# Row stage of a Hartley-transform convolution: from two column tiles of 64 rows to four of 32

## The reference

```python
# layer 0: a 3x3 filter whose taps come from the channel means, plus the input
lf = tanh(batchnorm(x.mean((2, 3)) @ conv_w.T)).reshape(N, G, 1, 9, 1)
low = sum(patches(x) * lf, axis=3).reshape(N, C, H, W)
x = (low * (inside_all + 1) - inside_all * gap) * lamb_l + x * (lamb_h + 1)
# layer 1: 20 x 20 modes of a 2-D Hartley transform, mixed over channels
x_ht = dht_2d(x)
out_ht[:, :, :20, :20] = compl_mul2d(x_ht[:, :, :20, :20], w1)
y = dht_2d(out_ht) / (H * W)
y = gaussian_smoothing_4d(y)      # 9 taps along images, channels, rows, columns
return y * (abs(fftfreq(W)) <= 0.25)
```

## Time and profile before

| | us |
|---|---|
| median of 3 runs | 151.3 |
| lowest and highest | 150.71 and 153.71 |
| the profiled execution, whole time | 152.74 |
| its span, first to last instruction | 150.9 |

### The profile page before, as it was taken

How to read it: one execution, slowest core, us unless ns; L and a number is a source line. 1 busy time by engine, 2 the same in 40 slices (tenths; PEclk the granted TensorE clock), 3 DMA queues, 4 the chain that set the end, 5 groups by cost and what they waited for, 6 DMA issues and landing times.

```text
span 150.9 us, 5209 instructions
## 1 busy us (share of the span) xinstructions
PE 125.7 (83%) x2308; PEld 71.9 (48%) x2308; DVE 79.8 (53%) x162; ACT 40.3 (27%) x92; POOL 55.3 (37%) x75
## 2 busy tenths in 40 slices
PE   6496558999999999999899797798797987999500
PEld 5132412655463626257567796465463654654200
DVE  0014840856497969595678114664846748444400
ACT  3000410011112020202599311343242423432300
POOL 8980000399876969699974000000000000000000
PEclk9999997589999999999999999999999999999995
DMA  3999999999999998000000000066998989999994
GB/s 99 358 359 321 295 347 362 348 349 372 371 363 380 351 351 273 11 2 4 0 2 0 4 4 4 4 213 242 312 365 300 384 300 329 350 376 380 386 386 158
DMA packets 34839, 37.04 MB, mean 245 GB/s; under 512 B 1162, under 2 KB 34260, under 8 KB 34816
## 3 DMA queue, kind: packets, MB, share of 16 engines
q1 hardware_dynamic: 34816, 36.70, 72.5%
HBM read 19.92 MB, written 16.78 MB: 243 GB/s over the span
## 4 chain that ended last, share of the span: by engine, by line
PE 28%; POOL 27%; DVE 13%; SPq 9%; DMA 9%; issue 8%; ACT 1%; POOLq 0%; DVEq 0%
PE ps L524 11%; POOL acc L870 5%; DMA x_ring<-x 5%; POOL rows L892 5%; SPq L315 5%; PE ps L464 4%; POOL spread L868 4%; PE ps L485 4%; DVE mixed L789 4%; PE ps L505 4%; DMA out<-rows 4%; DVE xht L726 4%; POOL row_prod L840 3%; POOL eo L878 2%; DVE rows L552 2%
## 5 line engine op out<-in xcount | busy, mean ns | idle before, releaser
L370 PE MATMUL ps<-x_ring,k_lt 64*64 64x512 f32 x256 | 34.7, 646 | 6.9 <-DMA x_ring<-x 6.9
L524 PE MATMUL ps<-cols,k_inv 128*64 128x330 f32 (+1 forms) x192 | 31.5, 466 | 4.5 <-DVE rows L552 4.0
L688 DVE STREAM_TRANSPOSE y_sb<-ps 128x1024 f32<-128x1024 f32 x16 | 19.5, 1241 | 18.2 <-PE ps L370 18.2
L524 PEld LDWEIGHTS ps<-cols,k_inv 128*64 128x64 f32 x192 | 13.3, 136 | 18.3 <-issue 11.8
L552 DVE COPY rows<-ps 128x330 f32<-128x330 f32 (+1 forms) x24 | 12.1, 522 | 12.1 <-PE ps L524 10.6
L388 PEld LDWEIGHTS ps<-y_sb,k_t 64*64 64x64 f32 x512 | 15.5, 143 | 5.0 <-DVE y_sb L688 2.7
L388 PE MATMUL ps<-y_sb,k_t 64*64 64x128 f32 x512 | 17.2, 288 | 0.4 <-ACT kb L589 0.4
L552 ACT COPY rows<-ps 128x330 f32<-128x330 f32 (+1 forms) x24 | 11.0, 462 | 23.7 <-PE ps L524 21.9
L370 PEld LDWEIGHTS ps<-x_ring,k_lt 64*64 64x64 f32 x256 | 8.7, 141 | 16.5 <-issue 9.1
L359 PE MATMUL ps<-idle 128*128 128x256 f32 x52 | 14.6, 431 | 1.2 <-DVE idle L657 1.2
L359 PEld LDWEIGHTS ps<-idle 128*128 128x128 f32 x52 | 10.5, 211 | 3.2 <-DVE idle L657 1.2
(11 more groups left out here) (70 smaller groups left out, 133.4 us busy)
## 6 DMA issues: line engine op xcount, KB each, us to landing
x_ring<-x SPq DMA_DIRECT2D x32, 512.0 KB, 8.7
out<-rows SPq DMA_DIRECT2D x16, 640.0 KB, 5.0
out<-rows SPq DMA_DIRECT2D x8, 768.0 KB, 6.2
w_sb<-mix_w SPq DMA_DIRECT2D x2, 960.0 KB, 10.1
k_inv<-inv SPq DMA_DIRECT2D x1, 386.0 KB, 8.6
k_t<-t SPq DMA_DIRECT2D x1, 256.0 KB, 7.2
k_basis<-basis SPq DMA_DIRECT2D x1, 240.0 KB
k_coef<-coef SPq DMA_DIRECT2D x4, 25.4 KB
```

The lines of the kernel that those rows point to most:

```text
L370: last = mm(ps[64 * m:64 * m + 64, 2 * hs + g, :], k_lt[64 * g:64 * g + 64, 64 * r:64 * r + 64], x_ring[64 * g:64 * g + 64, u, k:k + 4, r, ...
L524: last = mm(ps[64 * g:64 * g + 64, B_F[k % 3], 0:nt * NW], inv(O_LH + s * H + r * H // 2, (1, H // 2)), cols[:, u, 6 * g:6 * g + nt, :], s ...
L688: nc.vector.transpose(view(y_sb[:, n % 2, 0, 8 * hs, 0:1], (KINDS, 8), (KINDS * HC, 4), (1, 32)), view(ps[:, 2 * hs, 0:1], (1, 1024))).the ...
```

## The change

The row stage is cut four ways in place of two. A partition of `rows` now holds four image rows of 128 for each group of four channels. A chunk is made of four column tiles of 32 output partitions, one for each residue g of the channel number, and two halves (two image rows), so eight calls of `mm` in place of two, with half as many columns each: 3 x 66 = 198, or 2 x 66 = 132. The chunks become 396, 396, 396, 396, 264 and 264 columns, where they were 396, 396, 330, 330, 330 and 330. The tables, the order of the channels and the slices that `to_columns` takes follow the new layout; the copy has one dimension more. The stores are still three an image, of 3, 3 and 2 groups of four channels: 786, 786 and 524 KB, in runs of 2 KB.

```diff
-    order = np.arange(C).reshape(C // 2, 2).T.reshape(-1)
+    order = np.arange(C).reshape(C // 4, 4).T.reshape(-1)
-    wide[:, O_LH:O_TURN] = lh.reshape(3, 128, H // 2, 2).transpose(1, 0, 3, 2).reshape(128, -1)
+    wide[:, O_LH:O_TURN] = lh.reshape(3, 128, H // 4, 4).transpose(1, 0, 3, 2).reshape(128, -1)
-        rows = sb("rows", [128, 2, C // 2, 2, H])
+        rows = sb("rows", [128, 2, C // 4, 4, H])
-        CHUNKS = [(s, r, 6 if s == 0 else 5) for s in range(3) for r in range(2)]
+        CHUNKS = [(s, r, 3 if s < 2 else 2) for s in range(3) for r in range(2)]
-            out_pair = out.rearrange("n (k g) h w -> n k (g h w)", g=2).rearrange("n k (q e) -> n q k e", e=2 * H)
+            out_quad = out.rearrange("n (k g) h w -> n k (g h w)", g=4).rearrange("n k (q e) -> n q k e", e=4 * H)
-                    sp.dma_start(out_pair[n, :, s:HC:3, :],
-                                 rows[:, u, s:HC:3, :, :].rearrange("q k r w -> q k (r w)")
+                    sp.dma_start(out_quad[n, :, s:C // 4:3, :],
+                                 rows[:, u, s:C // 4:3, :, :].rearrange("q k r w -> q k (r w)")
-                    first = 3 * t * NF
+                    first = (t // 3 * 8 + t % 3 * 3) * NF
-                    for g in range(2):
-                        last = mm(ps[64 * g:64 * g + 64, B_F[k % 3], 0:nt * NW],
-                                  inv(O_LH + s * H + r * H // 2, (1, H // 2)),
-                                  cols[:, u, 6 * g:6 * g + nt, :], start=True, stop=True)
+                    for half in range(2):
+                        for g in range(4):
+                            last = mm(ps[32 * g:32 * g + 32, B_F[k % 3], half * nt * NW:(half + 1) * nt * NW],
+                                      inv(O_LH + s * H + (2 * r + half) * H // 4, (1, H // 4)),
+                                      cols[:, u, 3 * g:3 * g + nt, :], start=True, stop=True)
-            return copy(view(rows[:, u, s, r, 0:1], (3 * 2 * H, nt), (H - HALF, 2), (1, HALF)),
-                        view(ps[:, B_F[k % 3], 0:1], (NW, nt), (HALF, 2), (1, HALF)))
+            return copy(view(rows[:, u, s, 2 * r, 0:1], (H, 2), (3 * 4 * H, nt), (H - HALF, 2), (1, HALF)),
+                        view(ps[:, B_F[k % 3], 0:1], (nt * NW, 2), (NW, nt), (HALF, 2), (1, HALF)))
```

## The result

| | before | after |
|---|---|---|
| median of the runs, us | 152.24 (4 runs) | 164.44 (4 runs) |
| lowest and highest, us | 150.71, 153.71 | 162.62, 165.53 |
| span of the profiled execution, us | 150.9 | 162.3 |
| instruction packets | 18 | 22 |

The ratio is 1.085, with a 95% interval of 1.067 to 1.103: slower, as forecast, and 3 us beyond the range. The span grew by 11.4 us where the sum gave 6.4.

The account below looks back on a forecast made before the run. VectorE's chain (6.34 us an image) was taken as the bound until image 4, then the stores. With 7.8 us of PE stops, 145.2 + 8.5 + 3.6 gave a span of 157.3, median 157.7 us; range 152.3 to 161.5.

Parts of the forecast that it names:

- the sum: Whole kernel: last copy at 145.2, remaining stores 8.5, remainder 3.6, giving a span of 157.3 us, 6.4 over before.
- What bounds the kernel before: Inverse half: the chain through VectorE, 6.34 us an image, starves the stores (5.45 us) until image 4; then stores run solid.
- The runs of 2 KB: Output stores: 401 GB/s for 385, a gain of 0.7 us; rival that they don't help changes no verdict.
- The copy: VectorE's copy of a chunk: 570 ns at 396 columns for 498 at 330, +0.07 us on the chain.
- Four column tiles side by side: Row-stage matmuls on PE: four tiles overlap fully, so chunks 0 to 2 add only 0.12 us an image.
- The count: PE's instruction queue: 1152 more records, so 22 or 23 instruction packets for 18.
- mostly hidden: PE's borders between 256-instruction blocks: the skill's rule that they cost little, which would give a sum of 151.1 us.
- The walk: PE's block borders followed image by image from image 0's start: stops of 7.8 us in all.
- 4.4 us between blocks: PE's instruction fetch under stores: a block can start 4.4 us after the one before, bounds 3.7 and 5.
- the lower bound: PE's instruction fetch: 3.7 us between block starts (1.15 + 1.2 + 1.35); under stores too, the walk ends near 153.5.
- no stops at all: Rival on PE's instruction fetch: code comes far enough ahead, span 151.1, median 151.5, the same; chance 0.19.
- tiles in pairs: Rival on `to_rows`: four column tiles don't overlap with 128 rows, 8.5 us an image at least, about 167; chance 0.03.

Follow-up runs that it names:

- before_pool: Kernel before with the shares moved from VectorE to POOL, each as a multiply and an add: 149.5 us, ratio 0.987.
- after_1k: Changed kernel with each store cut across its runs into two DMAs of 1 KB runs, six an image: 159.8 us, ratio 1.048.
- after_cutk: Changed kernel with stores cut between groups of channels into eight DMAs an image, runs still 2 KB: 157.0 us, ratio 1.037.
- split4_cut: Kernel before with row-stage calls cut in four (48 an image) and stores cut into nine DMAs, 1 KB runs: 158.1 us, ratio 1.048.
- after_pool_cut: Changed kernel with the shares on POOL and the stores cut into eight DMAs an image: 156.3 us, ratio 1.036.
- pool_cut: Kernel before with the shares on POOL and the stores cut into nine DMAs an image: 150.0 us, ratio 0.993.
- after_bf16: Changed kernel with the operands of the row stage alone in bfloat16, one pass a call, lower output precision: 156.1 us.

## Why the prediction was right or wrong

**Right.** What bounds the kernel before: taking the shares off VectorE made it faster, and without stores its images still began 6.34 us apart. The runs of 2 KB: 400 GB/s for 401. The copy: 571 ns for 570. Four column tiles side by side: 2.22 us for 2.23. The count: 22 packets, and halts at most of the places named, 256 records or a multiple apart. The rule that I had set against the trace, that a border is "mostly hidden" (the Trainium skill, Runtime: NRT & Kernel Launch, "Instruction fetch mechanics"), fails here: the halts at borders make 9.3 us. The two blocks that the same section gives agree with the trace, in which every halt lies one block of 256 or a few behind the one before and ends some 1.35 us after a packet; by its other sentence, a buffer of 2048 instructions, and the reading in the prediction, no halt would have come.

**Wrong: the spacing of blocks under stores, the place of the halts, and a clock left out.** The mechanism, halts of PE at borders, was right; its size was not. The walk went border by border, so it can be held against the chain:

| halt in | predicted, us | measured, us |
|---|---|---|
| image 0, `to_columns` | 0.3 | 0.40 |
| image 1, record 14 | 0.5 | none |
| image 1, `turn` | 1.2 | 2.75 |
| image 2, last chunks | 2.1 | 0.68 |
| image 3, `turn` | 0 | 0.83 |
| image 4, record 34 | 0.3 | 0.12 |
| image 4, `turn` | 1.4 | 2.95 |
| image 5, last chunks | 2.0 | 0.66 |
| image 6, last chunks | 0 | 0.87 |

1. *The wait of a packet under stores.* I took 4.4 us between blocks, bounds 3.7 and 5. Measured: a packet began 0.7 to 3.95 us after its border, so 3.0 to 6.3 us between blocks. The upper bound was too low: the seven waits that the trace of before holds under stores all lay between 1.9 and 2.6, and its borders came mostly 6.0 to 6.3 us apart, about once an image, so that they fell at like places of it. A bound from samples taken at one phase is no bound; `before_pool`, with the same borders in shorter images, has 3.0 to 4.2. With the two long waits, the two halts in `turn` of images 1 and 4 came out 3.1 us longer than predicted.
2. *Where a halt falls.* One in the last chunks is partly covered, since PE would have waited for VectorE; one in `turn` is not, since the copy to `modes` and the shares stand behind it. I predicted 4.1 us in the covered places and 2.6 in `turn`; it came to 2.2 and 6.5. So it is not only the sum of the halts (9.3 for 7.8) that counts, but where they stand.
3. *The clock.* It was no term at all. After the halt of 2.75 us PE ran at 1.2 GHz to about 112.5, after the one of 2.95 to about 139.8 (the stretch shown above); there six chunks took 6.31 us for some 3.8. The first fall was hidden by VectorE's shares. The second put image 5 back by about 1.4 us, an estimate: VectorE's copy ended at 137.0, so at full clock three chunks of 2.22 would have ended at 139.4, and they ended at 140.75. No run separates this cost. In three kernels with 48 float32 calls whose halts stayed under 1.9 us (`after_1k`, `after_cutk`, `split4_cut`) the clock held in the profiled execution; in a fourth, `after_pool_cut`, it did not.

With these, image 6 began at 144.6 for 140.7, and the end followed, 162.3 for 157.3. The walk was also wrong the other way: at the lower bound, without stores, it gave some 4 us of halts for 1.1. Why it asks too much there stays open.

**Of the rivals**, no stops at all is out (every run with 48 calls has them), tiles in pairs is out (2.22 us), and the runs of 2 KB do help by their rate, as in the sum; but their gain is found in no time here, since the stores starve.

## What to carry to other kernels

Count the records of an engine between two points of the trace and set them against the instruction packets: where 256 of them pass in less than about 4 us (5 to 6 under large stores), this kernel halted at borders, whether or not its arithmetic would fit. Splitting a matmul into tiles that run side by side took no more PE time here (2.22 us for 2.23) and was not free in instructions; what it buys must be worth the supply. When a small transfer has to get through beside a stream, try cutting the stream's DMAs: here that gave back 7 of the 12 us by the medians (5 of 12 from the start of the row stage) where packets were late, and cost 1% where they weren't, through the issue of more DMAs. And before two profiles are compared, look whether they part ahead of the change: here up to 3.4 us did.

## What the runs showed of the hardware that I had not expected

- An instruction packet waited up to 4.5 us behind whole stores of 524 to 786 KB, and mostly under 2.7 us behind cut ones of 131 to 393 KB, with runs of 1 KB or 2 KB. One packet of `after_1k` waited 2.8 us and one of `after_pool_cut` 3.3, so this is no hard bound.
- From the end of a packet to PE's first instruction of its block: about 1.35 us, within some 0.2, at the halts of the kernels here.
- Issuing a store costs SP 0.4 to 0.5 us each time, in some cases over 1; with nine stores an image that was on the chain (`pool_cut`).
- In `after_bf16`, whose row stage takes one pass for two, the granted clock was at 1.2 GHz for the last 30 us: `to_columns` then took 1.5 us for 0.86, though nothing in it had changed.
